# A fused attention, mixture-of-experts and recurrence kernel on one core: 23 instead of 24 units for the sorted experts, seven recurrence steps in each, stages moved into the gaps between steps, and in the nine shared units behind them the remainders on VectorE and the gathers in a row on GpSimd

## The reference

```python
xn = layernorm(x)
x = x + linear_attention(xn) + moe_16_experts_top6(xn)     # layer 0
xn = layernorm(x)
x = x + recurrence(xn) + moe_8_experts_top2_plus_shared(xn) # layer 1
# recurrence: u = xn @ W_in.T + b_in ; s_t = tanh(u_t + s_(t-1) * gamma + beta) ; y = s @ W_out.T + b_out
# expert: (silu(h @ w_gate.T) * (h @ w_up.T)) @ w_down.T, width 176; the shared one is 352 wide
```

## Time and profile before

| | us |
|---|---|
| median of 3 runs | 677.58 (676.92 to 679.07) |
| the profiled execution | 680.39 |
| its span, first to last instruction | 678.8 |
| TensorE busy | 624.3 |
| VectorE busy | 448.0 |
| ScalarE busy | 369.1 |
| GpSimd busy | 247.4 |

### The profile page before, as it was taken

How to read it: one execution, slowest core, us unless ns; L and a number is a source line. 1 busy time by engine, 2 the same in 40 slices (tenths; PEclk the granted TensorE clock), 3 DMA queues, 4 the chain that set the end, 5 groups by cost and what they waited for, 6 DMA issues and landing times. The chain is left out here.

```text
span 678.8 us, 12642 instructions
## 1 busy us (share of the span) xinstructions
PE 624.3 (92%) x3607; PEld 343.8 (51%) x3607; DVE 448.0 (66%) x1519; ACT 369.1 (54%) x1008; POOL 247.4 (36%) x267
## 2 busy tenths in 40 slices
PE   6999899999999988999999989999877899888985
PEld 2665344544444434444454434454554576656754
DVE  7873876567943767674677775567682756774666
ACT  2445445456446456567556666746456647563550
POOL 5246222222242125532225523223610342653483
PEclk8999999999999999999999999999987899988998
DMA  8103577773495435852556620507322455752133
GB/s 305 60 1 132 188 247 242 246 233 95 141 341 188 153 104 173 267 185 96 177 187 209 218 93 1 214 11 123 87 38 63 93 143 129 174 153 77 40 113 99
DMA packets 91228, 99.06 MB, mean 146 GB/s; under 512 B 30478, under 2 KB 81774, under 8 KB 90734
## 3 DMA queue, kind: packets, MB, share of 16 engines
q10 hardware_dynamic: 45840, 46.40, 20.9%
q1 hardware_dynamic: 39950, 37.21, 19.0%
q0 software_dynamic: 5376, 14.69, 7.2%
HBM read 27.96 MB, written 64.03 MB: 136 GB/s over the span
## 5 line engine op out<-in xcount | busy, mean ns | idle before, releaser
L1876 POOL TENSOR_TENSOR hl<-scr,hh 128x512 f16<-128x512 f32 (+2 forms) x100 | 115.9, 1159 | 288.7 <-ACT hh L1265 287.1
L1295 ACT ACTIVATE RING<-zbuf 128x16 f32<-128x16 f32 x512 | 111.0, 217 | 149.6 <-DVE zbuf L1732 145.3
L714 PE MATMUL G<-xT,W 128*128 128x512 f16 (+2 forms) x600 | 146.3, 380 | 4.9 <-ACT scr L1257 2.9
L714 PE MATMUL U<-xT,W 128*128 128x512 f16 (+2 forms) x600 | 147.2, 382 | 2.7 <-DVE scr L1747 2.7
L1732 DVE TENSOR_TENSOR_SCAN zbuf<-C,RING 128x32 f32<-128x32 f32 x350 | 77.0, 220 | 76.1 <-ACT RING L1295 75.7
L714 PE MATMUL Y<-hh,W 128*128 128x512 f16 x352 | 119.3, 380 | 6.7 <-POOL hl L1876 6.6
L714 PEld LDWEIGHTS U<-xT,W 128*128 128x128 f16 (+3 forms) x600 | 61.4, 103 | 72.4 <-DVE scr L1747 4.0
L714 PEld LDWEIGHTS G<-xT,W 128*128 128x128 f16 (+3 forms) x600 | 60.1, 102 | 69.7 <-issue 5.1
L1753 DVE TENSOR_TENSOR U<-U,CS 128x512 f32<-128x512 f32 x88 | 60.4, 686 | 39.2 <-PE U L714 32.7
L1257 ACT ACTIVATE scr<-G 128x512 f32<-128x512 f32 (+2 forms) x100 | 58.8, 588 | 47.1 <-PE G L714 46.6
L1265 ACT ACTIVATE hh<-scr 128x512 f16<-128x512 f32 (+2 forms) x100 | 61.8, 618 | 28.8 <-DVE scr L1747 26.1
(11 more groups left out here) (195 smaller groups left out, 849.9 us busy)
## 6 DMA issues: line engine op xcount, KB each, us to landing
xrows<-zeros ACTq DMA_DIRECT2D x15, 1280.0 KB, 6.1
yrows<-zeros ACTq DMA_DIRECT2D x12, 1536.0 KB, 6.0
stage<-weights SPq DMA_DIRECT2D x20, 384.0 KB
yrows<-scr POOLq DMA_DIRECT2D x48, 128.0 KB
yrows<-zeros ACTq DMA_DIRECT2D x3, 1408.0 KB, 5.6
stage<-weights SPq DMA_DIRECT2D x14, 256.0 KB
parked<-RING SPq DMA_DIRECT2D x1, 3520.0 KB, 12.7
W<-parked SPq DMA_DIRECT2D x1, 3520.0 KB, 11.6
```

The lines of the kernel that those rows point to most:

```text
L714: last = nc.tensor.matmul(bank_, w(wp), act(ap), start=start and n == 0, stop=stop and n == count - 1)
L1295: nc.scalar.activation(RING[:, (t + 1) % RING_T, ::2], zbuf[:, 1::2], ACT.Tanh).then_inc(state_done, 1)
L1876: nc.gpsimd.tensor_tensor(hl[rows, a, :], h32[a][rows, :], hh[rows, a, :], ALU.subtract)\
```

## The change

- A group has 23 tiles, two groups 46, so there are 23 R units (3 to 25); the pair of unit 14 has the last tile of one group and the first of the other. An R unit makes seven steps instead of six (`UNIT_STEPS`), an S unit six as before; step 511 falls into unit 29. Last units are 26 to 34.
- A table `UNIT_GAPS` names what ScalarE (heads, input copies, the exponential, `rows`) or VectorE (tails) does right behind step i of unit u. It takes the splits of block 1 (before in the fronts of units 6 to 9) to units 1 to 4, those of block 2 (fronts of 21 to 24) to units 20 to 23, those of block 3 (fronts of 34 and 35) to units 30 to 33; in each the head stands behind step 3 and the tail behind step 5 (block 3: 2 and 4). The input copies stand behind steps 0 and 2 of units 7 and 8, the exponential behind step 4 of unit 6, the rows behind step 3 of unit 5. The matmuls of `inputs` stay in the fronts.
- `more_inputs` (VectorE waits for the inputs of block 3) moves from unit 12 to 10, `attend` of block 2 from 26 to 25, the adds from 32 to 31 and from behind the units to 34. `UNITS_HELD` becomes 0, 1, 2, 28, 29.
- In the last nine units the tails of S units are made by VectorE behind step 4 of the next unit (`late_tail_of`), not by GpSimd. Gathers 16 to 31 stand in a row in unit 29 (before: three a unit in 30 to 34, one in 35); combines come four a unit in units 31 to 33 and four at the end (before three in 32 and 33, ten at the end).

The diff, cut to its core:

```diff
 SLOTTED = 6
+UNIT_STEPS = {"S": SLOTTED, "R": SLOTTED + 1}
 GROUPS = ((0, 1), (2, 3))
 CAP = 2 * COLS
-TILES = 24
+TILES = 23
 REGION = E1 * CAP + TILES * P
...
 UNITS = ([("S", 0, g) for g in range(3)]
-         + [("R", group, q) for group in (0, 1) for q in range(TILES // 2)]
+         + [("R", 2 * r // TILES, r) for r in range(len(GROUPS) * TILES // 2)]
          + [("S", j, g) for j in (1, 2, 3) for g in range(3)])
 DENSE0 = BLOCKS * CH0
-HALF_TILES = TILES // 2
+PAIRS_OF_TILES = len(GROUPS) * TILES // 2
+assert len(GROUPS) * TILES == 2 * PAIRS_OF_TILES
...
         C = bank("C")
-        HT = (G, C)
+        HT = (C, G)
...
-        UNITS_HELD = (0, 1, 2, 30, 31, 32, 33)
+        UNITS_HELD = (0, 1, 2, 28, 29)
...
@@ -415,29 +418,31 @@
             1: [("scatter", (2, 2))],
             2: [("sum_copy", (3, Y[1])), ("scatter", (2, 3))],
             3: [("sum_turn", (3, Y[1]))],
-            5: [("shared_add", (0, Y[0])), ("norm_turn", (7, Y[1])), ("rows", (3, 0))],
-            6: [("logits", (7, Y[1][1])), ("rows", (3, 1)), ("split_states", (1, 0))],
-            7: [("inputs", (3, 0, Y[1])), ("exp", (7,)), ("split_states", (1, 1))],
-            8: [("inputs", (3, 2, Y[1])), ("split_states", (1, 2))],
-            9: [("rank", (3, Y[1][1])), ("split_states", (1, 3))],
-            10: [("scatter", (3, 0)), ("scatter", (3, 1))],
+            5: [("shared_add", (0, Y[0])), ("norm_turn", (7, Y[1]))],
+            6: [("logits", (7, Y[1][1]))],
+            7: [("inputs", (3, 0, Y[1]))],
+            8: [("inputs", (3, 2, Y[1]))],
+            9: [("rank", (3, Y[1][1]))],
+            10: [("more_inputs", (4,)), ("scatter", (3, 0)), ("scatter", (3, 1))],
             11: [("scatter", (3, 2)), ("scatter", (3, 3))],
-            12: [("more_inputs", (4,))],
             14: [("attend", (1, Y[1]))],
-            21: [("split_states", (2, 0))],
-            22: [("split_states", (2, 1))],
-            23: [("split_states", (2, 2))],
-            24: [("split_states", (2, 3))],
-            26: [("attend", (2, Y[1]))],
-            30: [("hold_gamma", (BLOCKS,))],
-            32: [("shared_add", (1, Y[1]))],
-            34: [("split_states", (3, 0)), ("split_states", (3, 1))],
-            35: [("split_states", (3, 2)), ("split_states", (3, 3))],
+            25: [("attend", (2, Y[1]))],
+            28: [("hold_gamma", (BLOCKS,))],
+            31: [("shared_add", (1, Y[1]))],
+            34: [("shared_add", (2, Y[0]))],
         }
-        GATHERS = {**{18 + n: (2 * n, 2 * n + 2) for n in range(8)}, 30: (16, 19), 31: (19, 22), 32: (22, 25),
-                   33: (25, 28), 34: (28, 31), 35: (31, 32)}
-        COMBINES = {**{19 + n: (2 * n, 2 * n + 2) for n in range(8)}, 32: (16, 19), 33: (19, 22)}
-        COMBINED_BEFORE = (0, 16, 22)
+        GATHERS = {**{18 + n: (2 * n, 2 * n + 2) for n in range(8)}, 29: (16, 32)}
+        COMBINES = {**{19 + n: (2 * n, 2 * n + 2) for n in range(8)}, 31: (16, 20), 32: (20, 24), 33: (24, 28)}
+        UNIT_GAPS = {(5, 3): ("rows", (3, 0)), (5, 5): ("rows", (3, 1)),
+                     (7, 0): ("input_copy", (3, 0, Y[1][0])), (7, 2): ("input_copy", (3, 1, Y[1][1])), (6, 4): ("exp", (7,)),
+                     (8, 0): ("input_copy", (3, 2, Y[1][0])), (8, 2): ("input_copy", (3, 3, Y[1][1])),
+                     **{(1 + c, 3): ("states_head", (1, c)) for c in range(KH)},
+                     **{(1 + c, 5): ("states_tail", (1, c)) for c in range(KH)},
+                     **{(20 + c, 3): ("states_head", (2, c)) for c in range(KH)},
+                     **{(20 + c, 5): ("states_tail", (2, c)) for c in range(KH)},
+                     **{(30 + c, 2): ("states_head", (3, c)) for c in range(KH)},
+                     **{(30 + c, 4): ("states_tail", (3, c)) for c in range(KH)}}
+        COMBINED_BEFORE = (0, 16, 28)
...
+        def unit_gap(u, gap, share):
+
+            name, args = UNIT_GAPS.get((u, gap), (None, ()))
+            if name in share:
+                share[name](*args)
...
+        LATE = DENSE0 + 26
+
+        def steps_to(u):
+
+            return STEPS * TICKS0 + sum(UNIT_STEPS[UNITS[m][0]] for m in range(u))
+
+        def group_of_pair(r):
+
+            return (2 * r + 1) // TILES
+
+        def pairs_of_groups(count, parity):
+
+            return (-(-TILES * count // 2) + 1 - parity) // 2
+
+        def tiles_of(table_):
+
+            return table_[0:1, :, :].rearrange("o g t -> o (g t)")
...
         def tail_through(n):
 
-            return (tile_tail, tile_pairs(n + 1)) if kind(n) == "R" else (htail_done, dense_units(n + 1))
+            if kind(n) == "R":
+                return tile_tail, tile_pairs(n + 1)
+            if n >= LATE:
+                return late_tail, dense_units(n + 1) - dense_units(LATE)
+            return htail_done, dense_units(n + 1)
...
             def load_tiles(r):
-                if r == 0 or r == HALF_TILES:
-                    group = r // HALF_TILES
+                group = group_of_pair(r)
+                if r == 0 or group > group_of_pair(r - 1):
                     sp.wait_ge(table_done, 2 * (group + 1))
                     sp.wait_ge(scattered, 16 * K1 * BATCH * len(GROUPS[0]) * (group + 1))
                 if r == 0:
...
-                pe.wait_ge(htail_done, dense_units(n + 1))
+                pe.wait_ge(*tail_through(n))
...
                     if j == 2:
-                        pe.wait_ge(tile_y, TILES)
+                        pe.wait_ge(tile_y, PAIRS_OF_TILES)
...
-                elif r == 1:
-                    pe.wait_ge(z_done, STEPS * TICKS0 + SLOTTED * 3)
+                    pe.wait_ge(z_done, steps_to(3))
...
+                    input_copy(j, c, pair[c - c0])
+
+            def input_copy(j, c, bank_):
+                act.wait_ge(u_done, KH * j + c + 1)
...
+            gaps = {"rows": rows, "input_copy": input_copy, "exp": exp, "states_head": split_states}
...
             def unit_step(u, i):
-                step(TICKS0, SLOTTED * u + i)
+                state_at(steps_to(u) + i)
+                unit_gap(u, i, gaps)
...
+            in_front = {name: stage_ for name, stage_ in share.items() if name != "inputs"}
...
-                unit_front(u, share)
+                unit_front(u, in_front)
...
-                unit_step(u, 5)
+                for i in range(5, UNIT_STEPS[kind(n)]):
+                    unit_step(u, i)
...
+            def late_tail_of(n):
+                a, rows = n % 2, slice(0, rows_of(n))
+                dve.wait_ge(hhead_done, dense_units(n + 1))
+                nc.vector.tensor_tensor(hl[rows, a, :], h32[a][rows, :], hh[rows, a, :], ALU.subtract).then_inc(late_tail, 1)
+
...
-                    step(TICKS0, SLOTTED * u + i, u in UNITS_HELD)
-                    if u in UNIT_WOVEN:
+                    scan_at(steps_to(u) + i, u in UNITS_HELD)
+                    if u in UNIT_WOVEN and i < SLOTTED:
                         name, block_, first, each = UNIT_WOVEN[u]
                         for part in range(each):
                             share[name](block_, first + each * i + part)
+                    unit_gap(u, i, {"states_tail": split_states})
...
                 unit_step(4)
+                if n > LATE:
+                    late_tail_of(n - 1)
                 if kind(n) == "R":
                     tile_gated_of(n, 1)
-                unit_step(5)
+                for i in range(5, UNIT_STEPS[kind(n)]):
+                    unit_step(i)
                 for i in range(*COMBINES.get(u, (0, 0))):
                     combine(i)
-            shared_add(2, Y[0])
+            late_tail_of(DENSE0 + len(UNITS) - 1)
             for i in range(COMBINED_BEFORE[2], K1 * BATCH * BLOCKS):
                 combine(i)
             shared_add(BLOCKS - 1, Y[1])
@@ -1917,9 +1968,8 @@
             def gather(i):
 
...
-                done = HALF_TILES // 2 * (j // 2 + 1)
-                for stored in y_stored:
-                    pool.wait_ge(stored, 32 * done)
+                for parity, stored in enumerate(y_stored):
+                    pool.wait_ge(stored, 32 * pairs_of_groups(j // 2 + 1, parity))
...
             for u in range(len(UNITS)):
                 n = DENSE0 + u
-                if kind(n - 1) != "R":
+                if kind(n - 1) != "R" and n <= LATE:
                     h_tail(n - 1, (n - 1) % 2)
                 unit_front(u, share)
+                for i in range(SLOTTED):
+                    unit_gap(u, i, {"rows": rows})
                 if u >= 3 and kind(n - 3) == "R":
                     store_tiles(tile_pairs(n - 3))
                 for i in range(*GATHERS.get(u, (0, 0))):
                     gather(i)
-            h_tail(DENSE0 + len(UNITS) - 1, (DENSE0 + len(UNITS) - 1) % 2)
```

39 lines of the change are left out of this document (20 added, 19 removed).

## The result

| | us |
|---|---|
| changed kernel, median of 4 runs | 667.57 (664.72 to 669.55) |
| kernel before beside it, median of 4 | 678.07 |
| ratio, 95% interval | 0.983 (0.980 to 0.986) |
| forecast | 672.3 (range 662 to 679) |
| profiled execution of the changed kernel, its span | 664.72, 663.1 |

Faster, as forecast, by 10.5 us where 5.3 were summed. The profiled execution is the fastest of the four, with a granted clock of 0.986 where the profiled one of before had 0.977; two of the four ran at 0.977 and 0.979 and took 669.0 to 669.6. So the trace of after flatters by some 4 us: 2.6 of them lie ahead of unit 0, 1.4 at the first shared unit.

The account below looks back on a forecast made before the run. TensorE was taken to bound units 14 to 18 and almost the end, the scan-tanh recurrence units 3 to 9 and 19 to 23. Terms of -1.9 and -3.4 gave -5.3 off median 677.58: 672.3 us, own range 668 to 677, overall 662 to 679.

Parts of the forecast that it names:

- What follows the last matmul, adds and stores, stays: After the last matmul: adds and stores unchanged; only 0.5 us to win, from combines that delayed the last adds.
- The remainders: Shared units: remainders on VectorE cost 0.66 us each, its debt is carried, TensorE's 2.8 us of waits go; stretch -2.9.
- Gathers in a row: Shared units: sixteen gathers take 20.3 us, last lands some two us before needed; if held, 673.5 us, chance 0.04.
- The seventh step: Recurrence, 0.50 us a step: plus 3.5 in units 3 to 9, 0.5 a unit in units 20 to 23.
- The splits in gaps: Block 1 splits: minus 8.4 us from fronts of units 6 to 9, plus 5.6 in gaps of units 1 to 4.
- Copies, exponential and rows: Units 5 to 8: copies and exponential moved from fronts to gaps, minus 5.0 us; rows in a gap, plus 0.9.
- Units 10 to 13: Their seventh steps ask 2.0 us; charged 1.2 because TensorE is close behind, bounds 0 and 2.0.
- The removed unit: After unit 24: three units and an attention, 16.8 us, become 13.6 with one unit fewer, minus 3.2.
- The sign posts: First scans: unit 10 near 534, 14 near 557, 20 near 582, 24 near 607, 26 near 620; also steps, waits.
- (b): Sorted units: the recurrence becomes the pace of all; 683 us at worst, 680.5 with two thirds; chance 0.10.
- (c): Whole kernel: nothing nets, half of the case where the recurrence paces all sorted units; 677.5 us, chance 0.10.
- (a): Gaps hide the work: units 20 to 23 fall to 4.5 us each, units 1 to 4 win more; 662, chance 0.20.

Follow-up runs that it names:

- the trace at the clock of before: Trace of the changed kernel with its sixteen late gathers issued three to a unit again, remainders still on VectorE; 668.85 us, ratio 0.985.

## Why the prediction was right in sign and half in size

The sum missed 5.2 of 10.5 us, and 667.57 lies below the forecast's own range of 668 to 677, in the part of 662 to 679 that was there for a rival. By its own steps, against the trace at the clock of before:

- **"What follows the last matmul, adds and stores, stays"** is the step that failed most: -0.5 against -2.85. The adds came 0.4 sooner behind the last matmul (0.24 us for 0.62), near the 0.5 that was summed, and the stores did stay; the other 2.5 is the DRAIN of GpSimd behind them, which was not looked for. Three experiments pin it: it ends 9.07 to 9.09 us after GpSimd's last instruction, whether that is a gather, a remainder or a memset.
- **The remainders** were right in kind: 2.9 of waits went, none came back, the debt of VectorE was carried. The stretch fell by 3.85, with 3.4 us at half clock in it both times. 1.8 of waits and 0.3 more return when the remainders go back to GpSimd; 1.7 don't, and so belong to the rest of the change. Of that 1.0 is the rest of the waits (2.8 against 1.8), 0.7 has no row.
- **Gathers in a row** were forecast to stay neutral, and did. Sixteen took 22.5 us, not 20.3, the two longest 1.63 and 1.77 beside a split's tail and a remainder on VectorE (in two later traces one took 2.23). A price of five times, which the prediction quoted against the change from the Trainium skill (SBUF — State Buffer, the section "A bandwidth-pool intuition that's wrong (but worth ruling out)"), isn't there: 1.77 against 0.95 is 1.9 times, the longest 2.3. The Trainium skill (same title, section "Who interferes with whom") infers that `tensor_tensor` leaves descriptor writing alone. The two longest gathers don't prove the contrary, since a `scalar_tensor_tensor` with two inputs in SBUF lay beside them too. But the gather at 631.11 had only a remainder beside it, a `tensor_tensor` with two inputs in SBUF, and took 1.17 where the next, with nothing beside it, took 0.95; in five other traces such a gather took 1.12 to 1.20 with some 0.3 us of overlap, in a sixth 0.98 with 0.1. So the trace disagrees by 0.2 us a gather.
- **The seventh step** in units 20 to 23 was priced at 0.50 and is worth 0.12 (5.87 against 5.75 a unit): +1.36 instead of +2.6 for the four. The prediction had read the loop of scan and tanh from an undisturbed step and applied it where VectorE's own order, a tail and two combines, covers the tanh. In units 3 to 8 it is 0.27 instead of 0.50.
- **The splits in gaps** of units 1 to 4 brought 1.2 where -8.4 + 5.6 = -2.8 was summed; those of 20 to 23 0.5. Copies, exponential and rows brought 2.6 to 3.9 of 4.1. With seven steps at 0.27 that is -1.2, -2.6 to -3.9, +1.9: -1.9 to -3.2 for units 0 to 9, measured -2.50. Two errors of opposite sign: that -3.4 came near is luck. (Before, 3.3 us more of this stretch ran at half clock.)
- **Units 10 to 13** were charged 1.2 for steps and fell by 0.3. By the rows GpSimd holds them, which no run tests: it issues eight scatters and a store in between, and ScalarE's copy in unit 12 waits for that store, before 2.36 us, after 0.53 (the steps fell into this wait):

```profile
547.78 0.60 ACT L1285 ACTIVATE scr<-Y 128x512 f32<-128x512 f32 x1 [2.36 <-DMA yrows<-scr]
```

```profile
541.13 0.60 ACT L1320 ACTIVATE scr<-Y 128x512 f32<-128x512 f32 x1 [0.53 <-DMA yrows<-scr]
```

- **The removed unit** was -4.06 against -3.2: unit 24 took 8.34 and not 9.2, since the attention's matmuls began (603.71) before the unit's seventh step (604.74); the last unit took 4.42, as summed. No run changes the number of units alone.
- **The sign posts** held where they told of mechanisms: a split unit has one step of 1.41 and two of 1.05 to 1.08; ScalarE doesn't wait for an input product before its copies; no TensorE wait behind the first shared product; the last gather is issued 27 us after unit 28 starts. The first scans came at 534.8, 556.3, 580.5, 604.0 and 616.7 at the clock of before: the first 0.8 us later than its sign post, the others 0.7 to 3.3 earlier.
- **Rivals.** (b) and (c), the recurrence as pace of all sorted units, did not come; (a), the gaps hide the work, did not either: units 20 to 23 got longer, and the range held for another reason than the one for which it reached so low, which is luck. Slips in their sums move nothing: two thirds of (b)'s 11 give 679.6 and not 680.5, half of it 677.8, and the upper bound of units 20 to 23 is +4.6.

Still open: why GpSimd's DRAIN takes 9 us, 0.7 us in the shared units, and what the removed unit is worth by itself.
